# Two-layer transformer kernel: the store of x1, the second root, the statistics and the rows of h in layer 2, and who issues two transfers at layer 1's opening

## The reference, cut to what matters

```python
x = layernorm(x + attention_with_lora(x))      # layer 1: rope, causal softmax, per-batch adapters
x = layernorm(x + ffn(x))                      # layer 2
# layer 1's output, after its LayerNorm, is called x1 below; layer 2's ffn:
residual = x1
a = rmsnorm(x1, ln1_w);  attn = attention(a)                     # causal, no rope
mod = 0.1 * tanh(attn @ A)
h = rmsnorm(x1, ln2_w)
gate = silu(h @ W_in.T + mod * (h @ A) @ B);  up = h @ W_up.T
return residual + (gate * up) @ W_down.T
# layernorm(v) = (v - mean) / sqrt(var + 1e-5);  rmsnorm(v, w) = v / sqrt(mean(v*v) + 1e-6) * w
```

## Time and profile before

| | us |
|---|---|
| three executions: median (lowest, highest) | 2783.93 (2775.04, 2787.33) |
| profiled execution: its own time | 2788.6 |
| its span in the profile | 2786.8 |
| busy: PE / DVE / ACT / POOL | 2629.9 / 1600.0 / 1325.7 / 667.9 |
| granted TensorE clock, mean | 0.98 |

### The profile page before, as it was taken

One profiled execution on the slowest core, in us unless ns is written; L12 is line 12 of the kernel. 1 busy time (PEld: TensorE's weight loads), 2 busy tenths in 40 slices (PEclk: granted clock), 3 DMA queues, 4 the chain that ended last, 5 costly groups with the idle time before them and its releaser, 6 DMA issues.

```text
span 2786.8 us, 40960 instructions
## 1 busy us (share of the span) xinstructions
PE 2629.9 (94%) x13584; PEld 2019.6 (72%) x13584; DVE 1600.0 (57%) x4341; ACT 1325.7 (48%) x2739; POOL 667.9 (24%) x535
## 2 busy tenths in 40 slices
PE   6999999999888999999999889999999999999998
PEld 5777777777566666666666647888888888888886
DVE  5777777777847788787787774222222423333333
ACT  3777777777734666666666674111111321111111
POOL 4556555556321322222222221000000000000000
PEclk9999999999889999999999979999999999999999
DMA  6565556665545664565554534111111311111100
GB/s 148 113 146 138 138 124 142 147 144 130 148 120 125 133 131 106 132 132 102 127 132 103 125 83 161 47 47 47 47 47 47 115 47 47 47 47 47 47 30 30
DMA packets 174634, 276.44 MB, mean 99 GB/s; under 512 B 29556, under 2 KB 53876, under 8 KB 173940
## 3 DMA queue, kind: packets, MB, share of 16 engines
q1 hardware_dynamic: 170884, 259.98, 39.1%
q0 software_dynamic: 2304, 12.58, 1.3%
q10 hardware_dynamic: 1264, 1.64, 0.2%
HBM read 97.03 MB, written 42.99 MB: 50 GB/s over the span
## 4 chain that ended last, share of the span: by engine, by line
PE 54%; DVE 9%; issue 3%; ACT 2%; DMA 2%; SPq 1%; POOL 0%; ACTq 0%; DVEq 0%; POOLq 0%
PE lin_ps L2575 13%; PE b_scores_ps L2586 13%; PE b_pv_ps L2556 6%; PE b_scores_t_ps L2556 6%; PE lin_ps L2104 5%; PE b_pv_ps L311 2%; DVE b_prob L294 2%; DVE b_junk L206 2%; PE b_scores_t_ps L275 2%; PE lin_ps L2067 2%; PE b_scores_ps L192 1%; DMA b_k_stack<-b_k_split 1%; PE lin_ps L2581 1%; PE b_scores_ps L2049 1%; SPq L262 1%
## 5 line engine op out<-in xcount | busy, mean ns | idle before, releaser
L286 ACT ACTIVATE b_prob<-b_scores_t_ps 128x384 fp32r<-128x384 f32 (+1 forms) x384 | 201.1, 524 | 218.1 <-PE b_scores_t_ps L277 198.9
L294 DVE TENSOR_TENSOR a_prob<-a_scores_t_ps,a_prob 128x384 fp32r<-128x384 f32 (+1 forms) x384 | 225.3, 593 | 135.7 <-ACT a_scores_t_ps L287 134.2
L294 DVE TENSOR_TENSOR b_prob<-b_scores_t_ps,b_prob 128x384 fp32r<-128x384 f32 (+1 forms) x384 | 225.8, 592 | 100.1 <-ACT b_scores_t_ps L287 100.0
L286 ACT ACTIVATE a_prob<-a_scores_t_ps 128x384 fp32r<-128x384 f32 (+1 forms) x384 | 201.7, 525 | 156.4 <-PE a_scores_t_ps L277 130.8
L311 PE MATMUL b_pv_ps<-b_prob,b_value 128*33 128x512 f32 (+3 forms) x1024 | 273.6, 336 | 0.1
L311 PE MATMUL a_pv_ps<-a_prob,a_value 128*65 128x512 f32 (+3 forms) x1024 | 271.1, 333 | 0.4 <-DVE a_prob L294 0.2
L206 DVE CUSTOM_DVE_ANT_0 b_junk<-b_scores_ps,spare 128x512 bf16<-128x512 f32 (+3 forms) x512 | 226.8, 483 | 66.3 <-PE b_scores_ps L192 63.8
L206 DVE CUSTOM_DVE_ANT_0 a_junk<-a_scores_ps,spare 128x512 bf16<-128x512 f32 (+3 forms) x512 | 226.6, 483 | 26.9 <-PE a_scores_ps L192 24.8
L2519 DVE TENSOR_TENSOR res<-b_scores_ps,b_first_gate 128x512 f32<-128x512 f32 x64 | 44.3, 692 | 331.9 <-PE b_scores_ps L2586 331.9
L2519 DVE TENSOR_TENSOR stage<-b_scores_ps,b_junk 128x512 f32<-128x512 f32 x64 | 44.3, 692 | 328.2 <-PE b_scores_ps L2586 328.2
L1143 PE MATMUL lin_ps<-x_split,w_split 128*128 128x512 f32 x768 | 216.7, 397 | 1.5 <-DVE w_split L938 1.2
(11 more groups left out here) (318 smaller groups left out, 5908.8 us busy)
## 6 DMA issues: line engine op xcount, KB each, us to landing
a_q_stack<-a_q_split SPq DMA_DIRECT2D x192, 128.0 KB, 3.4
a_k_stack<-a_k_split SPq DMA_DIRECT2D x192, 128.0 KB, 3.5
b_q_stack<-b_q_split SPq DMA_DIRECT2D x192, 128.0 KB, 3.1
b_k_stack<-b_k_split SPq DMA_DIRECT2D x192, 128.0 KB, 3.7
spare<-h_t SPq DMA_DIRECT2D x16, 1024.0 KB, 6.2
stage<-in_x_t SPq DMA_DIRECT2D x8, 1024.0 KB, 6.5
a_sum_hi<-a_pv_raw SPq DMA_DIRECT2D x32, 256.0 KB, 3.8
a_inverse_all<-softmax_sums SPq DMA_DIRECT2D x32, 256.0 KB, 3.5
```

Of the source, the lines that this page charges most:

```text
L286: act.activation(at.prob_hi[:, k % at.ring, 0:w], at.scores_t_ps[:, k % 2, 0:w], ACT.Exp, scale=SCALE)
L294: dve.tensor_tensor(at.prob_lo[:, k % at.ring, 0:w], at.scores_t_ps[:, k % 2, 0:w], at.prob_hi[:, k % at.ring, 0:w], ALU.subtract).then_in ...
```

## The change

In the opening, `send_b(0)` and `send_low(0)` are issued by SP behind all the loads instead of by ACT; wv is split by ACT before it copies the first projections, and its low part is made by DVE instead of POOL. In layer 2, the statistics move one subtraction later, the second root is started from var*(1 + 1e-6) + 1e-11 and needs neither the first's reciprocal nor a product at the end (three instructions of 128x4 fewer for each batch), the subtraction of unit 11 of step 1 goes ahead of the two tiles of h, `normalise_tile` moves to step 3 slots 6 to 9, and `store_x1` to the end of SP's step 3, behind the last stacks.

```diff
@@ layer 1, SP
                 if n == 1:
                     constants()
+            sp.wait_ge(rows_zeroed, 2)
+            send_b(0)
+            send_low(0)
             for pair in range(2):
                 stack_send(sp, at, 0, 0, pair)
@@ layer 1, POOL
+            pool.wait_ge(const_in, 80)
...
-            pool.wait_ge(w_ready, 2 * KC)
-            for c in range(KC):
-                pool.wait_ge(w_hi, 2 * KC + c + 1)
-                pool.tensor_tensor(w_split[2][:, 1, c, :], w_stage[2][c], w_split[2][:, 0, c, :],
-                                   ALU.subtract).then_inc(w_ready, 1)
-            pool.wait_ge(const_in, 80)
@@ layer 1, ACT
             adapter(0)
-            act.wait_ge(rows_zeroed, 2)
-            act.wait_ge(ab_ready, 2)
-            for r, part in enumerate((0, 1, 0)):
-                act.dma_start(b_stack[RANK * r:RANK * (r + 1), :, :].bitcast(F32),
-                              b_split[:, part, :].bitcast(F32)).then_inc(b_stacked, 16)
             weights(0)
             low(0)
-            weights(1)
-            act.wait_ge(low_ready, 1)
-            for r, part in enumerate((0, 0, 1)):
-                act.dma_start(low_stack[RANK * r:RANK * (r + 1), :, :].bitcast(F32),
-                              low_split[:, part, :].bitcast(F32)).then_inc(low_stacked, 16)
+            for n in range(1, 3):
+                weights(n)
             for i in range(2):
                 projected(0, 0, i)
-            weights(2)
@@ layer 1, DVE
             constants()
+            weights(2)
@@ layer 2, SP step
                     gather(*group(b, g, -1))
-                if g == 3 and not last:
-                    store_x1(b + 1)
...
                     stack_send(sp, at, *group(b, g, 2), 1)
+                if g == 3 and not last:
+                    store_x1(b + 1)
@@ layer 2, DVE
-        LN_STEPS = TT + 5 + RSQRT_STEPS
+        LN_STEPS = TT + 2 + RSQRT_STEPS
...
                 dve.tensor_tensor(res[:, t, :], lin_ps[:, t % 2, :], res[:, t, :], ALU.add).then_inc(o_added, 1)
+
+            def statistics(b, t):
                 dve.wait_ge(o_added, b * TT + t + 1)
                 dve.bn_stats(stats[:, t, :], res[:, t, :]).then_inc(stats_done, 1)
...
                 dve.tensor_scalar(squares[:, 0, :], mean_var[:, :, 1], LN_EPS, None, ALU.add).then_inc(ln_step, 1)
-                dve.wait_ge(ln_step, done + TT + 1)
-                dve.reciprocal(newton[:, 0, :], squares[:, 0, :]).then_inc(ln_step, 1)
-                dve.wait_ge(ln_step, done + TT + 2)
-                dve.tensor_tensor(newton[:, 1, :], newton[:, 0, :], mean_var[:, :, 1], ALU.mult).then_inc(ln_step, 1)
-                dve.wait_ge(ln_step, done + TT + 3)
-                dve.tensor_scalar(squares[:, 1, :], newton[:, 1, :], RMS_EPS, None, ALU.add).then_inc(ln_step, 1)
+                dve.tensor_scalar(squares[:, 1, :], mean_var[:, :, 1], 1.0 + RMS_EPS, LN_EPS * RMS_EPS, ALU.mult,
+                                  ALU.add).then_inc(ln_step, 1)
...
-            def both_roots(b):
-                dve.wait_ge(ln_step, b * LN_STEPS + TT + 4 + RSQRT_STEPS)
-                dve.tensor_tensor(inv_root[:, 1, :], inv_root[:, 0, :], inv_root[:, 1, :], ALU.mult).then_inc(ln_step, 1)
...
                 for slot in range(UNITS):
+                    if slot > 0:
+                        lo_unit(dve, at, b, g, slot - 1)
+                    elif g == 2 and not last:
+                        for t in range(2):
+                            h_rows(b + 1, t)
+                    elif not first:
+                        lo_unit(dve, at, *group(b, g, -1), UNITS - 1)
+                    if g == 0 and slot == 11 and not last:
+                        statistics(b + 1, 0)
+                    if g == 1 and slot in (2, 8, 10) and not last:
+                        statistics(b + 1, 1 + (2, 8, 10).index(slot))
                     if g == 1 and slot == 10 and not last:
                         variances(b + 1)
-                    if slot > 0:
-                        lo_unit(dve, at, b, g, slot - 1)
-                    elif not first:
-                        lo_unit(dve, at, *group(b, g, -1), UNITS - 1)
...
                             for i in range(1, 3):
                                 root_round(b + 1, i)
-                            both_roots(b + 1)
-                            h_rows(b + 1, 0)
-                            h_rows(b + 1, 1)
+                            lo_unit(dve, at, b, g, slot)
...
                     if g == 2 and not last:
-                        if slot >= UNITS - TT:
-                            normalise_tile(b + 1, slot - (UNITS - TT))
...
                         for to in left_b(b, g, slot - 1):
                             projected(*to)
+                    if g == 3 and 6 <= slot < 6 + TT and not last:
+                        normalise_tile(b + 1, slot - 6)
```

More of the change, by code:

```diff
@@ L1857, in variances @@
                 dve.tensor_scalar(squares[:, 0, :], mean_var[:, :, 1], LN_EPS, None, ALU.add).then_inc(ln_step, 1)
-                dve.wait_ge(ln_step, done + TT + 1)
-                dve.reciprocal(newton[:, 0, :], squares[:, 0, :]).then_inc(ln_step, 1)
-                dve.wait_ge(ln_step, done + TT + 2)
-                dve.tensor_tensor(newton[:, 1, :], newton[:, 0, :], mean_var[:, :, 1], ALU.mult).then_inc(ln_step, 1)
-                dve.wait_ge(ln_step, done + TT + 3)
-                dve.tensor_scalar(squares[:, 1, :], newton[:, 1, :], RMS_EPS, None, ALU.add).then_inc(ln_step, 1)
+                dve.tensor_scalar(squares[:, 1, :], mean_var[:, :, 1], 1.0 + RMS_EPS, LN_EPS * RMS_EPS, ALU.mult,
+                                  ALU.add).then_inc(ln_step, 1)
             def root_start(b):
-                done = b * LN_STEPS + TT + 4
+                done = b * LN_STEPS + TT + 2
                 dve.wait_ge(ln_step, done)
@@ L1870, in root_round @@
             def root_round(b, i):
-                rsqrt_round(dve, ln_step, b * LN_STEPS + TT + 4, inv_root[:, :, :], squares[:, :, :], newton[:, :, :], i)
-            def both_roots(b):
-                dve.wait_ge(ln_step, b * LN_STEPS + TT + 4 + RSQRT_STEPS)
-                dve.tensor_tensor(inv_root[:, 1, :], inv_root[:, 0, :], inv_root[:, 1, :], ALU.mult).then_inc(ln_step, 1)
+                rsqrt_round(dve, ln_step, b * LN_STEPS + TT + 2, inv_root[:, :, :], squares[:, :, :], newton[:, :, :], i)
             def h_rows(b, t):
@@ L1988, in step @@
                             projected(*to)
+                    if g == 3 and 6 <= slot < 6 + TT and not last:
+                        normalise_tile(b + 1, slot - 6)
             for t in range(TT):
                 add_residual(0, t)
+                statistics(0, t)
             variances(0)
@@ L1995, in _ @@
                 root_round(0, i)
-            both_roots(0)
             dve.wait_ge(vw_made, 2)
```

## The result

The kernel after takes 2795.64 us in the median of 6 executions (2794.14 to 2797.66), the kernel before 2784.22 in 6 (2775.04 to 2787.33). The ratio is 1.0047, 95% interval 1.0036 to 1.0057: 11.4 us slower, where 4.1 less was forecast and 2791 was the top of the range. The profiled execution of after has a span of 2793.2 us against 2786.8, 6.4 more.

The account below looks back on a forecast made before the run. PE, busy for 94% of the span, was taken to bound the kernel. The terms -3.1 - 0.6 - 3.2 - 3.8 + 9.6 - 3.0 summed to -4.1 us, for a forecast of 2779.5 us, range 2768 to 2791.

Parts of the forecast that it names:

- the tiles: Layer 2, step 3 slots 6 to 9: idle DVE carries the moved tiles; if not, at most 0.45 us a tile.
- the store: Layer 2, step 0: x1's store delays the gather 2.1 us, costing 1.6 in six batches, +9.6 us.
- batch 7: Layer 2's batch 7: weight loads start behind the gather, so PE's waits nearly go, -3 us.
- the k stack: Layer 2, out of step 2: without the tiles k is ready earlier, 0.55 us in seven batches, -3.8 us.
- the opening: Layer 1's start: ropes without POOL beside them save 3.4 us, transfers cost 0.3, -3.1 us.
- the slower one: Rival, step 0: gather's delay and late splits pass on whole, 3.5 us a batch, +14, 2798; chance 0.08.
- Steps 1 to 2: Layer 2: the new DVE order gains 0.45 us in each of seven batches, not 2.4, -3.2 us.
- the rival of the late rows: Rival, opening: low rows land 3 us late on SP's queue, eating the gain; -1 in all, 2783; chance 0.12.

Follow-up runs that it names:

- e4: The kernel after with the store of x1 between the rows of b and the low rows in SP's step 3: 2781.20 us, 0.9988 of before.
- e2: The kernel before with, in layer 2, only the second root, later statistics and unit 11's subtraction ahead of h: 2789.61 us, 1.0011 of before.
- e5: e4 with POOL's first sum in step 2 waiting for all four of DVE's low parts of h: 2777.05 us, 0.9962 of before.
- e6: e4 with all four tiles of x1 in slot 9 of step 3: 2774.70 us, 0.9956 of before.
- e1: The kernel before with only the change of layer 1's opening: 2781.86 us against 2785.66, ratio 0.9998.
- e9: e7 with the opening's six transfers (rows of b, low rows) on ACT's queue again: 2773.57 us, 0.9957 of before.
- e10: e8 with only the opening's six transfers moved from ACT's queue to SP's: 2774.79 us, 0.9956 of before.
- e8: e7 with layer 1's opening as in before: 2771.55 us, 0.9944 of before.
- e12: e8 run once more, with the old opening: 2774.53 us, 0.9958 of before.
- e3: The kernel before with only x1's tiles and its store moved as in after: 2792.94 us, 1.0030 of before.
- e7: e4 with the edits of both e5 and e6: 2770.91 us, 0.9944 of before; run again 2771.67 us, 0.9954.

## Why the prediction was wrong

**Wrong in the sign of the whole**, by three terms of the sum. By the traces, after is 6.4 us longer and not 4.1 shorter. Of these 10.5 us the collision in step 2 makes 8.2, the tiles 5.4, the store 4.2, the reordering and batch 7 1.4; the k stack (6.0) and the opening (3.3) gave more than forecast, and 0.6 is the rest.

*"The store of x1 ... I take 1.6 us for 2.1".* The mechanism was right, and e4 shows it. The size was off: 13.8 us instead of 9.6. Both factors were too low. The gather landed 1.6 to 3.8 us later, 2.5 in the mean of six batches, for 2.1; and step 0 grew by 1.6 to 3.6, 2.4 in the mean, which is 0.94 us for each us of delay and not 1.6/2.1 = 0.76. A fixed delay of 2.0 to 2.3 assumed that the store's data are all that the gather stands behind, but the issues of its last two transfers also took 1.41 and 1.48 us in place of 0.6; that the queue was full is my reading, no run shows it. And in batch 4 the wait was followed by a lower clock. The place was wrong too: not the shift's turn in slot 8, for which PE never waits in these six batches, but the subtraction of unit 5 behind ACT's exponential, for which it waits ahead of slot 7. Of the rivals, the slower one was nearest (2798), but by chance: it needed 3.5 a batch from the store alone.

*"Steps 1 to 2 ... What a batch gains is thus not 2.4 but 0.45".* That reading was right in the main: PE waits 0.44, 0.56 and 0.19 before slots 0, 1 and 2 of step 2, about as drawn, and the seven batches gave 2.2 for 3.2. Two details were not. The wait ahead of slot 11 did not close, and the waits of slot 9 do not return in each batch within 0.1 us: before has none in batches 0 and 3 and 0.6 in 4 and 6. The step that failed is that I stopped there and put nothing down for the rest of step 2. With the subtraction of unit 11 earlier, step 2's gather is issued 0.8 us earlier into the step too, and this releases POOL's sum onto DVE's low part of h: +8.2 us, nearly four times what the edit gave. The prediction followed each engine's own list and never asked what the earlier landing would start, and beside what. e2 shows it alone, e5 takes it away.

*"In step 3 the four tiles (2 us) lie in slots 6 to 9, ahead of an idle stretch of DVE ... If that cover is gone, they cost at most 0.45 a tile".* The cover wasn't there, and the price was too low. The idle stretch begins behind slot 9; the tiles of slots 6 to 8 stand before subtractions that PE waits for, and the first of them took up to 2.09 us, not 0.45, beside POOL. The 0.45 was read from the tile of slot 10, which meets no instruction of POOL; that of slot 8 met one already in before. +5.4 us; e6 brings it to zero.

The other terms: *the k stack* gave 9.8 for 3.8. The waits of 8.4 us went nearly whole, as SP no longer waited for a k that stands behind tiles. Some 3 to 4 us of it is a draw of this one execution of before: behind its waits of 2.40 and 1.84 the clock had fallen, and e1 and e2, with the same tiles and the same store, already show 3.3 and 4.1 us less in those slots. In *the opening* the ropes and the low rows did as drawn, and the trace gained more than 3.1. But the sum put the 3.4 us to the ropes and a charge of 0.3 to the transfers, and e9 and e10 show that the one gives 1.1 without the other, since the ropes start on time only if wv lands early; the rival of the late rows didn't come (the last of them lands at 25.0 to 26.8 us on SP's queue, at 26.3 to 26.6 on ACT's); and of the whole e8 to e12 leave 0.6 and 2.9 us in the time. *Batch 7* gave 2.6 for 3.0, and its step 0 2.9, for the reason given: its wait for the k stack (1.77 in before) is gone, and that for the shift is 0.42 for 1.46. The total is partly chance: from one execution to another batch 7 differs by several us where nothing in it was changed (2.1 less than before in e12, 2.2 more in e9).

The Trainium skill, page "SBUF — State Buffer" (section "SBUF: two separate sides", the shared port pair), says that a GpSimd instruction and a VectorE one that has two SBUF inputs or runs in a two-port mode hold the pair for a whole instruction, and the later one waits; it counts `tensor_scalar`, as x1's tile is, among the operations that can enter such a mode. The traces agree. Each of the five hindered low parts of h in after ends 0.54 to 0.55 us after POOL's instruction does, and each of the six hindered tiles 0.28 to 0.29 after it; unhindered they take 0.69 and 0.54. One meeting fits less well: at layer 2's start in e1 a low part of h takes 1.00 us (811.0 to 812.0) wholly inside one POOL instruction (810.7 to 812.8), without waiting for its end. I had used that rule where the change removed such a meeting (the opening) and not where it made two.

## What to carry to other kernels

When an edit makes a stage start earlier, list what its transfers release, on every engine, and what will then run beside it: here 0.8 us of earlier landing cost more than the edit gained. A large store belongs where its queue is idle and nobody waits behind it; the place was visible as a wait of 4.8 us on SP (1055.9 to 1060.6 in after, and the same in before). Price a wait of PE with what the clock does behind it, not by its length alone.

## What I had not expected of the hardware

The granted clock fell to its lower level for 3 us, once 7, behind idle stretches of PE of only 1.5 us between busy ones (batch 1, windows above: 0.50, then 0.68). The length of the stretch alone doesn't decide it. Ahead of slot 5 of step 2, where the collisions are, a wait of 1.44 to 1.79 us was followed by a fall in 11 of 18 cases (after, e2, e4, e6). Ahead of slot 1 of step 2, in the kernels with the old order (before, e1, e3), a wait of 1.40 to 1.43 us was followed by none in 21. What sets the two apart isn't shown. In e7 to e12, from 860 to 1570 us, PE's longest wait was 0.89 us and the clock never fell. Such falls make single executions differ by several us (29 executions of before beside e1 to e4 run from 2779.7 us at a mean clock of 0.982 to 2794.0 at 0.977), so that a part worth 3 us can't be read from one trace.

The meetings with POOL end alike in all traces that have them: where a POOL instruction ends inside a low part of h, that 128x512 subtraction ends 0.54 to 0.55 us after it, and where one ends inside a tile of x1, the tile ends 0.28 to 0.34 after it.

A moved subtraction or a moved transfer acts at a distance: with the opening's transfers on SP's queue the first scores came up to 4.9 us earlier and the last of layer 2's units 5.1 earlier than in e8 (e7), though layer 2 began 7.2 earlier. Those 2 us went in step 0 of batches 1 to 6 (+2.2 in all), where e7 waits 2.0 for the shift's row; why these waits come is open.
